# A written-out order of steps is replaced, and idle matmuls are put ahead of three stages

## The chip, the cores and the metric

One Trainium2 chip, and on it one core. A core has five engines that each run their own instruction stream in order: TensorE (PE, matmuls), VectorE (DVE), ScalarE (ACT), GpSimd (POOL) and SyncE (SP, which issues most transfers). They meet through semaphores. The metric is device time in microseconds of one execution; the median of three runs of the kernel before is 534.73 us (533.21 to 534.82).

## The reference

x has 2048 tokens of 128 features (4 batches of 512). Three layers act on it: half of a mixture of experts, a linear attention, and half of the same mixture again.

```python
x = x + 0.5 * ffn(layernorm(x)); x = x + attn(layernorm(x)); x = x + 0.5 * ffn(layernorm(x))

def ffn(x):    # 8 experts, 2 of them per token
    logits = (x @ gate_w + gate_b) / 0.9
    probs = softmax(logits where among the top 2, else -inf)
    h = gelu(einsum('bsd,edf->bsef', x, w1) + b1)             # 128 -> 512
    y = einsum('bse,bsed->bsd', probs, einsum('bsef,efd->bsed', h, w2) + b2)
    return layernorm(y) * ln_g + ln_b

def attn(x):   # 16 heads of 64, feature map elu + 1
    q, k, v = x @ wq + bq, x @ wk + bk, x @ wv + bv
    qm, km = elu(q) + 1, elu(k) + 1
    kv, z = einsum('nshd,nshm->nhmd', km, v), 1 / (einsum('nlhd,nhd->nlh', qm, km.sum(1)) + 1e-6)
    return einsum('nlhm,hmf->nlf', einsum('nlhd,nhmd,nlh->nlhm', qm, kv, z), wo) + bo
```

## The kernel before

The whole order of work is one list of words, ORDER (lines 65 to 113). A word is a step: its kind, then its arguments, where f1 is the first FFN, att the attention and f2 the second FFN. Each engine goes through the same list in the same order and takes from each step what is its part; so a word that moves, moves the step's instructions on every engine that has some, its DMA issues on SyncE among them. No scheduler stands behind it.

The tokens are worked on in four tiles of 512. In each FFN one tile is "dense": all eight experts are computed for it, as 16 units of half an expert (up.0 to up.15 and down.0 to down.15 in the first FFN, units 54 to 69 in the second). The other three tiles are "sparse": their tokens are scattered into blocks of 256 by expert, in DRAM (sorted1 and sorted2), and a block is one unit (units 16 to 34, and 35 to 53); a block beyond an expert's first gets its weights by a copy from W into Wd1 and Wd2, by a table made at run time. Results go to DRAM, and a gather brings two per token back.

A unit runs through four engines. xb: transposes of a loaded block on PE, a high part on ACT, a low part on DVE (matmuls are done in three products of high and low parts). up: 12 matmuls (6 in a dense unit), then the gelu on ACT, for dense units also the copy hh. low: DVE's low part hl. down: 12 matmuls (6) into one of two halves of psB. For a sparse unit then DVE's add of b2 (yT), yt: transposes on PE, a copy to yb on ACT, the store on SP. yb has two buffers, so ACT's copy of a unit waits for the store of the unit two before (L1088 to L1093), and down of a unit waits for the copy of the unit two before, which frees its half of psB (wait_bank, L707). mix: DVE adds a dense expert's gated result to acc.

Weights come in as stages: step W.u loads expert u's w1 and w2 (W.8 and W.9: wq and wk) into one of two stage buffers on SP; ACT copies the high part, Wl.u makes the low part on DVE, and only then may the stage after next be loaded. wv and wo load what is folded into VW. mix.u on SP reloads pb, the gate weights of the expert after next, once DVE's mix.u has freed it. fill1 (issued on ACT's queue) and fill (on SP) write zeros to sorted1 and sorted2. For fill, DVE first clears tok:

```python
sp.wait_ge(zero_ready, 2)
sp.dma_start(xs[1]..., zrow.unsqueeze(1).to_broadcast([P, 16, ROWS2 // 16])).then_inc(filled[1], 16)
```

The attention runs batch by batch: K.n.i and Q.n.j (products on PE, exponentials on ACT, Kf and Qf on DVE), kt and ksum (the sum of keys), kv (keys times normalised x, in psB), kvout (its copy, ACT), G (with VW), den and denz (the reciprocal of the denominator, DVE), z (spread over the heads by a matmul on zq), qz (DVE), out, oT, att. Between them stand, for tiles 1 to 3, the end of the first FFN (gather on POOL, top1 on ACT, comb, fstat and finish on DVE), the statistics of the next layernorm (stats on DVE, their root on POOL, norm on ACT), and the routing of the second FFN (gate, logits, top, route, slots, scatter). psA has two slots that up, K, Q, G, z, oT and some small steps use in turn.

On PE, SP and ACT the stores and copies of units 16 to 34 and the start of the attention stand so:

```python
act.wait_ge(y_stored[s % 2], 16 * (s // 2))     # L1092, step yt: ACT's copy to yb
pe.wait_ge(yb_ready, sparse_no(prior) + 1)      # L712, wait_bank: ahead of down
```

A kernel starts with 12 matmuls of ident on itself into psB (WARM_UP, L717), whose result is not used.

Of the kernel before, what the change touches and what calls it, by code (L numbers as in the profile page):

```python
# [69 lines left out]
top.f1.1.2 top.f1.1.3 route.f1.1.D low.4 consts picks down.2 scatter.f1.0 mix.1 table.f1 prep scatter.f1.1 scatter.f1.2  # L70
scatter.f1.3 scatter.f1.4 scatter.f1.5 scatter.f1.6 scatter.f1.7 scatter.f1.8 scatter.f1.9 scatter.f1.10 up.5 scatter.f1.11
exp.f1.1 W.5 Wl.4 low.5 wv down.3 slots.f1.1 up.6 mix.3 wo down.4 low.6 up.7 wvT.0.C W.6 Wl.5 up.8 down.5 mix.5 low.7 low.8 up.9
down.6 W.7 Wl.6 down.7 wvT.1.C mix.7 low.9 up.10 VW.0.C down.8 low.10 W.8 down.9 VW.1.C Wl.7 low.11 up.11 mix.9 up.12 VW.2.C
down.10 low.12 up.13 W.9 down.11 Wl.8 up.14 VW.3.C mix.11 low.13 down.12 low.14 up.15 Wl.9 down.13 bvwo.0.C mix.13 low.15
down.14 bvwo.1.C down.15 mix.15 xb.16 xb.17 up.16 xb.18 kbias low.16 up.17 xb.19 accT.f1.C shift.f1.0 fstat.f1.0 low.17 up.18
down.16 low.18 xb.20 up.19 xb.21 down.17 yt.16 low.19 up.20 finish.f1.0 xb.22 yt.17 down.18 stats.att.0 low.20 up.21 xb.23
norm.att.0 yt.18 low.21 up.22 down.19 xT.att.0.C down.20 xb.24 xl.att.0 yt.19 up.23 xb.25 low.22 soft.f1.1 down.21 yt.20 low.23
up.24 xb.26 shift.f1.1 down.22 yt.21 low.24 up.25 yt.22 down.23 xb.27 low.25 up.26 xb.28 shift.f1.2 down.24 yt.23 low.26 up.27
down.25 yt.24 xb.29 low.27 yt.25 up.28 xb.30 shift.f1.3 down.26 low.28 up.29 xb.31 up.30 yt.26 down.27 low.29 down.28 xb.32
yt.27 low.30 up.31 xb.33 yt.28 low.31 down.29 up.32 xb.34 yt.29 low.32 up.33 down.30 down.31 yt.30 low.33 down.32 up.34 yt.31  # L80
low.34 K.0.0 down.33 yt.32 down.34 yt.33 yt.34 gather.f1.1.0 gather.f1.1.1 K.0.1 gather.f1.1.2 gather.f1.1.3 Kf.0.0 fill Q.0.0
Kf.0.1 kt.0.1 kv.0.0 K.0.2 Qf.0.0 Kf.0.2 kt.0.2 Q.0.1 kv.0.1 K.0.3 Qf.0.1 Q.0.2 kv.0.2 Q.0.3 Kf.0.3 kt.0.3 Qf.0.2 Qf.0.3 kv.0.3
kvout.0 ksum.0 comb.f1.1 gs.0 top1.f1.1 fstat.f1.1 finish.f1.1 den.0.0 den.0.1 denz.0 stats.att.1 gather.f1.2.0 gather.f1.2.1
G.0 norm.att.1 z.0.0 qz.0.0 z.0.1 xT.att.1.A xl.att.1 qz.0.1 out.0.0 z.0.2 z.0.3 qz.0.2 K.1.0 out.0.1 gather.f1.2.2 qz.0.3
out.0.2 K.1.1 Kf.1.0 gather.f1.2.3 Kf.1.1 kt.1.1 outc.0 K.1.2 out.0.3 kv.1.0 top1.f1.2 comb.f1.2 fstat.f1.2 gather.f1.3.0 kv.1.1
K.1.3 Kf.1.2 kt.1.2 Q.1.0 Kf.1.3 kt.1.3 kv.1.2 Q.1.1 finish.f1.2 stats.att.2 gather.f1.3.1 Qf.1.0 Q.1.2 Qf.1.1 norm.att.2
gather.f1.3.2 gather.f1.3.3 Qf.1.2 Q.1.3 ksum.1 xT.att.2.A xl.att.2 Qf.1.3 gs.1 att.0 oT.0 K.2.0 top1.f1.3 comb.f1.3 den.1.0
kv.1.3 K.2.1 Kf.2.0 fstat.f1.3 K.2.2 finish.f1.3 Kf.2.1 kt.2.1 den.1.1 kv.2.0 stats.att.3 denz.1 stats.f2.0 kv.2.1 Kf.2.2 Kf.2.3
kvout.1 K.2.3 G.1 kt.2.2 kt.2.3 norm.att.3 xT.att.3.A xl.att.3 norm.f2.0 Q.2.0 z.1.0 qz.1.0 kv.2.2 z.1.1 qz.1.1 z.1.2 Qf.2.0
out.1.0 Q.2.1 qz.1.2 out.1.1 Qf.2.1 xl.f2.0 Q.2.2 z.1.3 qz.1.3 out.1.2 Qf.2.2 xT.f2.0.A Q.2.3 gate.f2.0.A logits.f2.0 out.1.3  # L90
top.f2.0.0 top.f2.0.1 kv.2.3 outc.1 Qf.2.3 top.f2.0.2 kvout.2 top.f2.0.3 route.f2.0.A slots.f2.0 scatter.f2.0 scatter.f2.1 K.3.0
Kf.3.0 ksum.2 gs.2 oT.1 att.1 scatter.f2.2 stats.f2.1 exp.f2.0 scatter.f2.3 den.2.0 den.2.1 denz.2 K.3.1 norm.f2.1 soft.f2.0
Kf.3.1 kt.3.1 K.3.2 kv.3.0 Kf.3.2 xl.f2.1 kv.3.1 xT.f2.1.A kt.3.2 G.2 K.3.3 z.2.0 qz.2.0 Kf.3.3 kt.3.3 qz.2.1 out.2.0
logits.f2.1 z.2.1 gate.f2.1.A out.2.1 z.2.2 qz.2.2 kv.3.2 top.f2.1.0 z.2.3 Q.3.0 qz.2.3 Q.3.1 out.2.2 out.2.3 outc.2 Qf.3.0
top.f2.1.1 top.f2.1.2 top.f2.1.3 route.f2.1.A Qf.3.1 oT.2 att.2 slots.f2.1 stats.f2.2 scatter.f2.4 scatter.f2.5 Q.3.2 Qf.3.2
scatter.f2.6 scatter.f2.7 Q.3.3 norm.f2.2 shift.f2.0 ksum.3 gs.3 kv.3.3 Qf.3.3 xT.f2.2.A xl.f2.2 den.3.0 kvout.3 gate.f2.2.A
logits.f2.2 den.3.1 top.f2.2.0 denz.3 G.3 top.f2.2.1 top.f2.2.2 scatter.f2.8 scatter.f2.9 scatter.f2.10 scatter.f2.11 z.3.0
top.f2.2.3 route.f2.2.A slots.f2.2 qz.3.0 z.3.1 qz.3.1 out.3.0 table.f2 dest.f2 exp.f2.1 exp.f2.2 outc.3 qz.3.2 out.3.1 z.3.2
z.3.3 qz.3.3 out.3.2 shift.f2.1 shift.f2.2 out.3.3 soft.f2.1 soft.f2.2 xb.35 xb.36 up.35 xb.37 low.35 up.36 xb.38 oT.3 att.3
up.37 low.36 xb.39 low.37 up.38 down.35 stats.f2.3 xb.40 low.38 down.36 yt.35 up.39 xb.41 norm.f2.3 down.37 yt.36 xb.42 low.39  # L100
up.40 yt.37 xl.f2.3 down.38 xT.f2.3.C low.40 up.41 down.39 yt.38 low.41 gate.f2.3.C xb.43 logits.f2.3 up.42 top.f2.3.0
top.f2.3.1 down.40 xb.44 low.42 up.43 yt.39 xb.45 top.f2.3.2 top.f2.3.3 exp.f2.3 up.44 yt.40 down.41 low.43 xb.46 soft.f2.3
shift.f2.3 down.42 yt.41 low.44 up.45 xb.47 probsT.f2.C down.43 yt.42 up.46 xb.48 low.45 yt.43 down.44 low.46 up.47 xb.49
down.45 yt.44 low.47 up.48 yt.45 low.48 down.46 xb.50 up.49 yt.46 xb.51 down.47 low.49 up.50 yt.47 xb.52 down.48 low.50 up.51
yt.48 xb.53 low.51 down.49 up.52 down.50 yt.49 low.52 down.51 yt.50 low.53 pb.f2 up.53 up.54 down.52 yt.51 low.54 up.55 down.53
yt.52 low.55 yt.53 up.56 down.54 low.56 up.57 gather.f2.0.0 gather.f2.0.1 gather.f2.0.2 gather.f2.0.3 down.55 mix.55 low.57
up.58 down.56 low.58 up.59 down.57 mix.57 gather.f2.1.0 low.59 up.60 top1.f2.0 comb.f2.0 down.58 low.60 up.61 gather.f2.1.1
gather.f2.1.2 fstat.f2.0 gather.f2.1.3 down.59 mix.59 up.62 low.61 finish.f2.0 gather.f2.2.0 gather.f2.2.1 gather.f2.2.2
gather.f2.2.3 mix.61 store.0 down.60 low.62 up.63 top1.f2.1 comb.f2.1 fstat.f2.1 down.61 low.63 up.64 low.64 up.65 store.1
down.62 low.65 down.63 mix.63 finish.f2.1 up.66 low.66 top1.f2.2 comb.f2.2 fstat.f2.2 down.64 up.67 down.65 mix.65 low.67  # L110
# [1542 lines left out]
```

## Time and profile before

| what | us |
|---|---|
| median of three runs | 534.73 |
| the profiled execution, its own time | 535.36 |
| its span, first to last instruction | 533.6 |
| PE busy | 423.0 (79%) |
| DVE busy | 364.1 (68%) |
| ACT busy | 277.0 (52%) |
| POOL busy | 165.7 (31%) |
| zero fill of sorted2 (7552 KB), issue to landing | 24.4 |

The profile is of one execution. Busy time counts matmuls, vector and scalar instructions; waiting is what lies between. PEclk is the share of full speed that TensorE's clock was granted: 1.00 is 2.4 GHz, 0.50 is 1.2 GHz, and a stretch in between held both. In a row of a timeline, the square brackets give how long the engine sat idle before the instruction and what ended that.

### The profile page before, as it was taken

Reading aid. Unit: us, or ns where it says so; the run is one execution under the profiler, and the core shown is the slowest. Engines: PE = TensorE matmul, PEld = TensorE weight load, DVE = VectorE, ACT = ScalarE, POOL = GpSimd, SP = SyncE. Lnnn points to the kernel's source line nnn. Section 1 sums busy time; section 2 is a strip of 40 time slices with the busy share of each in tenths; the row PEclk is TensorE's granted clock in tenths of the full one; section 3 lists DMA queues with packets and bytes.
Section 4 is the critical chain, followed back from the end, with each engine's and each line's share of the span. In section 5 each row is a group of like instructions: output and inputs, shape, how many; then the busy total and the mean of one; then the engine's idle time right before and its main releaser. Section 6 shows DMA issues by size and latency. Waiting matters only on the chain.

```text
span 533.6 us, 8029 instructions
## 1 busy us (share of the span) xinstructions
PE 423.0 (79%) x2559; PEld 335.2 (63%) x2559; DVE 364.1 (68%) x790; ACT 277.0 (52%) x560; POOL 165.7 (31%) x253
## 2 busy tenths in 40 slices
...
GB/s 172 77 79 267 193 124 128 110 250 126 235 256 174 88 371 251 25 15 11 31 0 1 1 31 11 0 11 35 84 209 215 225 230 234 119 76 73 80 79 20
DMA packets 50816, 62.92 MB, mean 118 GB/s; under 512 B 7772, under 2 KB 36821, under 8 KB 50775
## 3 DMA queue, kind: packets, MB, share of 16 engines
...
q14 instruction: 21, 0.16, 0.1%
...
## 4 chain that ended last, share of the span: by engine, by line
PE 24%; issue 18%; DVE 15%; POOL 10%; ACT 4%; DMA 2%; SPq 1%; POOLq 0%; DVEq 0%; ACTq 0%
POOL g L1592 4%; POOL sorted L1577 3%; PE psA L703 3%; PE psC L963 3%; PE psA L705 3%; PE psA L704 3%; PE psB L703 2%; PE psB L705 2%; PE psB L704 2%; DVE bst L1179 2%; POOL rstd L1559 2%; PE psB L914 2%; DVE hl L1354 2%; DVE hh L1351 1%; DMA results<-yb 1%
## 5 line engine op out<-in xcount | busy, mean ns | idle before, releaser
L1354 DVE TENSOR_TENSOR hl<-hid,hh 128x1024 fp32r<-128x1024 f32 x70 | 86.2, 1234 | 25.0 <-ACT hh L1086 19.9
L1079 ACT ACTIVATE hid<-psA,cols 128x512 f32<-128x512 f32 (+1 forms) x128 | 66.1, 580 | 21.9 <-PE psA L705 16.7
L1577 POOL DMA_INDIRECT sorted<-tok,di x48 | 49.6, 1033 | 72.8 <-DVE di L1329 59.3
L703 PE MATMUL psB<-hh,W 128*128 128x512 f32 (+1 forms) x128 | 47.9, 374 | 10.9 <-DVE hl L1354 9.8
L1592 POOL DMA_INDIRECT g<-results,di x24 | 27.2, 1135 | 65.2 <-DMA results<-yb 57.9
L1557 POOL TENSOR_SCALAR ve<-mv 128x4 f32<-128x4 f32 x20 | 7.0, 349 | 128.7 <-DVE mv L1182 128.1
L704 PE MATMUL psB<-hl,W 128*128 128x512 f32 (+1 forms) x128 | 45.0, 352 | 0.0
L705 PE MATMUL psB<-hh,W 128*128 128x512 f32 (+1 forms) x128 | 44.6, 349 | 0.0
L1592 POOL DMA_INDIRECT g<-results,dy x24 | 26.6, 1107 | 54.9 <-DMA results<-yb 48.0
L1079 ACT ACTIVATE hid<-psA,cols_d 128x256 f32<-128x256 f32 x88 | 34.7, 478 | 15.8 <-PE psA L705 11.2
L703 PEld LDWEIGHTS psB<-hh,W 128*128 128x128 f32 x128 | 25.7, 201 | 17.4 <-DVE hl L1354 13.1
L963 PE MATMUL psC<-qm,Gs 128*128 128x512 f32 x64 | 33.3, 658 | 4.1 <-DVE qm L1503 4.1
L1102 ACT ACTIVATE X<-psA,less 128x1024 f32<-128x1024 f32 x16 | 17.8, 1113 | 35.9 <-PE psA L895 35.9
L1086 ACT CAST hh<-hid 128x1024 fp32r<-128x1024 f32 x32 | 33.6, 1049 | 2.6
L1111 ACT ACTIVATE X<-psA,cols 128x512 f32<-128x512 f32 x32 | 22.1, 690 | 24.3 <-PE psA L705 23.1
L914 PE MATMUL psB<-km,xn 128*128 128x512 f32 x64 | 30.1, 598 | 3.6 <-DVE km L1452 2.4
L1339 DVE TENSOR_TENSOR xbl<-psC,xbh 128x256 fp32r<-128x256 f32 x38 | 16.0, 420 | 22.0 <-ACT xbh L1056 21.8
L703 PE MATMUL psA<-xh,W 128*128 128x512 f32 x64 | 28.0, 437 | 3.8 <-DVE xl L1230 3.4
L1351 DVE CAST hh<-hid 128x1024 fp32r<-128x1024 f32 x38 | 27.6, 727 | 4.0 <-ACT hid L1079 4.0
L703 PE MATMUL psB<-hh,Wd 128*128 128x256 f32 x88 | 26.8, 304 | 1.9 <-issue 1.8
L705 PEld LDWEIGHTS psB<-hh,W 128*128 128x128 f32 x128 | 25.6, 200 | 3.2
L1452 DVE SCALAR_TENSOR_TENSOR km<-X,psA 128x1024 f32<-128x1024 f32 x16 | 19.3, 1214 | 11.9 <-ACT X L1102 11.7
...
## 6 DMA issues: line engine op xcount, KB each, us to landing
Wd<-W SPq DMA_DIRECT2D x44, 512.0 KB, 3.1
sorted<-tok SPq DMA_DIRECT2D x1, 7552.0 KB, 24.4
...
```

Source lines behind the costliest of these rows:

```text
L703: nc.tensor.matmul(o, ah, bh, start=start, stop=False)
L704: nc.tensor.matmul(o, ah, bl, start=False, stop=False)
L705: return nc.tensor.matmul(o, al, bh, start=False, stop=stop)
L914: last = nc.tensor.matmul(psB[:, j, :], xn[:, n % 2, i, :], km[:, ti % 2, j * BANK:(j + 1) * BANK], start=(i == 0), stop=(i == ST - 1))
L963: last = nc.tensor.matmul(psC[:, 1, :], Gs[:, c, :], qm[:, c, :], start=(c == 0), stop=(c == HP - 1))
L1079: last = nc.scalar.activation(hid[:, u % 2, q * width:(q + 1) * width], ps(st)[:, q * width:(q + 1) * width], ACT.Gelu, bias=bias)
L1086: nc.scalar.copy(hh[:, u % HS, :], hid[:, u % 2, :]).then_inc(hh_ready, 1)
L1111: nc.scalar.activation(X[:, fslot(k), cs], ps(st)[:, cs], ACT.Exp, bias=bias)
L1351: link(nc.vector.tensor_copy(hh[:, u % HS, :], hid[:, u % 2, :]))
L1354: nc.vector.tensor_tensor(hl[:, u % HS, :], hid[:, u % 2, :], hh[:, u % HS, :].bitcast(F32), ALU.subtract)\
L1577: nc.gpsimd.indirect_dma_start(xs[ix(r)], bass.IndirectOffsetOnAxis(di[:, ix(r), k, j:j + 1], 0), tok[:, j, :], None)\
L1592: nc.gpsimd.indirect_dma_start(g[:, v, 2 * t + k, :], None, ys[ix(r)], bass.IndirectOffsetOnAxis(slots[:, k, off(r, n) + t:off(r, n) + t + ...
```

## The change

ORDER is replaced as a whole: the same words in another order, but for six new ones, heat.-1.0, heat.-1.1, heat.0.0, heat.0.1, heat.3.0 and heat.3.1. A heat step issues matmuls on PE whose result nobody reads: 6 of ident on itself (n = -1), or 4 of 512 columns with expert 0's weights (n = 0 and 3), into the second half of psB. For n of 0 or more it waits until kvout has read psB.

```diff
 ORDER = """
-W.0 stats.f1.0 norm.f1.0 W0.0 bias.A W0.1 xT.f1.0.C stats.f1.1 W.1 norm.f1.1 stats.f1.2 xl.f1.0 route_consts stats.f1.3
+W.0 stats.f1.0 W0.0 bias.A norm.f1.0 stats.f1.1 W0.1 W.1 stats.f1.2 xl.f1.0 stats.f1.3 norm.f1.1 xT.f1.0.C heat.-1.0 heat.-1.1
...
-    return [(kind, *(stages[v] if v in stages else int(v) if v.isdigit() else v for v in a))
+    return [(kind, *(stages[v] if v in stages else int(v) if v.lstrip('-').isdigit() else v for v in a))
...
+                elif kind == "heat":
+
+                    n, _ = a
+                    if n >= 0:
+                        pe.wait_ge(kxT_ready, n + 1)
+                        for _ in range(4):
+                            nc.tensor.matmul(psB[:, 1, :], W[:, 0, 0, 0, 0:P], W[:, 0, 1, 0, :], start=True, stop=True)
+                    else:
+                        for _ in range(6):
+                            nc.tensor.matmul(psB[:, 1, 0:P], ident[:, :], ident[:, :], start=True, stop=True)
```

SP at the end of the first FFN's sparse blocks, before: L692 is the store of a unit's result (step yt), L600 the load of a unit's second weights, L628 the fill, L554 the load of the second FFN's first block.

```order
L692 DMA results1<-yb 128x2x128 x3
L600 ISA
L600 DMA Wd2<-W 128x1024
L692 DMA results1<-yb 128x2x128 x5
L628 DMA sorted2<-tok 2048x1x944
L554 DMA xb<-sorted2 128x2x128
```

The same place now:

```order
L692 DMA results1<-yb 128x2x128
L600 ISA
L600 DMA Wd2<-W 128x1024
L692 DMA results1<-yb 128x2x128
L628 DMA sorted2<-tok 2048x1x944
L692 DMA results1<-yb 128x2x128 x5
L554 DMA xb<-sorted2 128x2x128
```

The fill has moved ahead of the last five stores, those of units 30 to 34. On DVE its memset of tok stands behind unit 34's xb.

SP in the first dense series, before, from the reload that takes the gate table: L652 is pb.0, L617 and L618 are a stage's w1 and w2 (W.4, then W.5), L658 a reload of pb (step mix), L631 wv, L636 wo.

```order
L652 DMA pb<-gate_table 128x512 x2
L617 DMA stage<-in_L_ffn_w_dram 128x512
L618 DMA stage<-in_L_ffn_w_dram 128x4x128
L658 DMA pb<-gate_table 128x512
L617 DMA stage<-in_L_ffn_w_dram 128x512
L618 DMA stage<-in_L_ffn_w_dram 128x4x128
L631 DMA wv_sb<-in_L_attn_wv_dram 128x1024
```

The same place now:

```order
L652 DMA pb<-gate_table 128x512 x2
L631 DMA wv_sb<-in_L_attn_wv_dram 128x1024
L617 DMA stage<-in_L_ffn_w_dram 128x512
L618 DMA stage<-in_L_ffn_w_dram 128x4x128
L617 DMA stage<-in_L_ffn_w_dram 128x512
L618 DMA stage<-in_L_ffn_w_dram 128x4x128
L658 DMA pb<-gate_table 128x512
```

W.5 has moved ahead of mix.1's reload, and wv ahead of W.4. On ACT, W.4 and W.5 stand behind the gelu of units 4 and 5.

DVE where the last routing of the second FFN meets batch 3's denominator, before: L1248 is the first step of top, L1489 to L1496 denz.3, L1434 G.3, L1250 to L1252 the second step of top.

```order
L1248 TENSOR_REDUCE gm<-gL 128x4
L1489 TENSOR_SCALAR oT<-psC 128x128
L1491 RECIPROCAL oT<-oT 128x128
L1492 CAST zh<-oT 128x128
L1496 SCALAR_TENSOR_TENSOR zq<-zh,lower,oT 32x128 x4
L1434 TENSOR_TENSOR Gs<-psA,Gs 128x1024
L1250 TENSOR_TENSOR gS<-gA,gm 128x32
L1251 SCALAR_TENSOR_TENSOR gX<-gS,gL 128x32
```

The same now, where lines behind the new branch have numbers larger by 10: L1336 to L1339 are the last rows of slots, L1499 to L1506 denz.3, L1444 G.3, L1513 qz, L1297 the table.

```order
L1336 TENSOR_REDUCE gm<-gX 128x4
L1338 CAST di<-gm 128x4
L1339 CAST di<-gm 128x4
L1499 TENSOR_SCALAR oT<-psC 128x128
L1501 RECIPROCAL oT<-oT 128x128
L1502 CAST zh<-oT 128x128
L1506 SCALAR_TENSOR_TENSOR zq<-zh,lower,oT 32x128 x4
L1444 TENSOR_TENSOR Gs<-psA,Gs 128x1024
L1513 TENSOR_TENSOR qm<-qm,psA 128x1024 x2
L1297 TENSOR_TENSOR gX<-pos,steps 128x40
```

All of top, route and slots has moved ahead of denz.3 and G.3.

## Rows read from the trace of the kernel before

**Rows 1.** Windows by stage: length, busy time of each engine, clock, DMA share, GB/s.
```profile
core 0: us, PE busy (x) PEld busy (x) DVE busy (x) ACT busy (x) POOL busy (x), PEclk, DMA share, GB/s
17.77:99.81 82.04, 67.32 (x309) 53.58 (x310) 56.83 (x117) 48.60 (x66) 40.85 (x108) 0.87 0.49 152
99.81:172.41 72.60, 60.67 (x473) 58.22 (x472) 56.25 (x101) 40.70 (x110) 13.25 (x11) 0.95 0.57 192
184.26:362.22 177.96, 144.14 (x814) 95.06 (x817) 112.82 (x244) 89.26 (x181) 58.51 (x69) 0.93 0.16 59
362.22:389.87 27.65, 15.69 (x116) 8.88 (x116) 20.04 (x70) 0.95 (x2) 13.42 (x15) 0.88 0.19 66
465.60:533.60 68.00, 45.48 (x185) 34.56 (x183) 45.25 (x106) 36.48 (x55) 31.61 (x32) 0.90 0.23 66
```

**Rows 2.** Waits of ACT, 17 to 100 us: total, times, longest.
```profile
ACT W L992 <- DMA stage<-in_L_ffn_w_dram: 18.7, 4, 7.6
```

**Rows 3.** Timeline of ACT, 34 to 60 us: start, length, instruction, idle before.
```profile
40.88 1.05 ACT L992 CAST W<-stage 128x1024 fp32r<-128x1024 f32 x1 [6.19 <-DMA stage<-in_L_ffn_w_dram]
...
54.15 1.04 ACT L992 CAST W<-stage 128x1024 fp32r<-128x1024 f32 x1 [7.62 <-DMA stage<-in_L_ffn_w_dram]
```

**Rows 4.** Timeline of PE around the first z product and batch 1's G.
```profile
206.67 1.97 PE L933 MATMUL psA<-VW,kxT 128*64 128x128 f32 x32
215.93 1.19 PE L952 MATMUL psA<-zq,pick 128*128 128x512 f32 x2 [7.29 <-DVE zq L1496]
...
281.81 3.58 PE L933 MATMUL psA<-VW,kxT 128*64 128x128 f32 x32 [2.58 <-DVE km L1452]
```

**Rows 5.** Timeline of POOL, 364 to 386 us.
```profile
371.86 0.96 POOL L1577 DMA_INDIRECT sorted<-tok,di  x1 [5.94 <-DVE di L1329]
```

**Rows 6.** Timeline of SP's issues, 355 to 394 us.
```profile
383.04 0.39 SPq L554 DMA_DIRECT2D xb<-sorted  x1
384.23 0.52 SPq L582 DMA_DIRECT2D Wd<-W  x1
384.88 0.51 SPq L587 DMA_DIRECT2D cols_d<-cols_e  x1
```

**Rows 7.** Timeline of SP's issues, 30 to 50 us.
```profile
35.51 0.43 SPq L617 DMA_DIRECT2D stage<-in_L_ffn_w_dram  x1
...
47.85 0.46 SPq L617 DMA_DIRECT2D stage<-in_L_ffn_w_dram  x1
```

**Rows 8.** Page, part 6: transfers, KB each, median us from issue to landing.
```profile
Wd<-W SPq DMA_DIRECT2D x44, 512.0 KB, 3.1
sorted<-tok SPq DMA_DIRECT2D x1, 7552.0 KB, 24.4
...
cols_d<-cols_e SPq DMA_DIRECT2D x22, 2.5 KB, 2.5
```

**Rows 9.** Timeline of PE, 0 to 18 us.
```profile
1.75 4.60 PE L718 MATMUL psB<-ident 128*128 128x128 f32 x24 [1.75 <-POOLq L1525]
...
17.77 0.77 PE L703 MATMUL psA<-xh,W 128*128 128x512 f32 x1 [3.41 <-DVE xl L1230]
```

**Rows 10.** Timeline of SP's issues, 160 to 190 us.
```profile
174.43 10.87 SPq L692 DMA_DIRECT2D results<-yb  x5
186.16 0.64 SPq L628 DMA_DIRECT2D sorted<-tok  x1
```

**Rows 11.** Timeline of DVE, 262 to 284 us.
```profile
266.38 1.23 DVE L1391 SCALAR_TENSOR_TENSOR g<-g,pr 128x128 f32<-128x128 f32 x4 [3.51 <-ACT g L1009]
```

**Rows 12.** Timeline of DVE, 355 to 386 us.
```profile
363.36 0.29 DVE L1489 TENSOR_SCALAR oT<-psC 128x128 f32<-128x128 f32 x1
...
367.53 0.18 DVE L1250 TENSOR_TENSOR gS<-gA,gm 128x32 f32<-128x32 f32 x1
```

**Rows 13.** Timeline of DVE, 500 to 534 us.
```profile
506.77 1.14 DVE L1421 SCALAR_TENSOR_TENSOR x<-g,rstd,x 128x128 f32<-128x128 f32 x4 [1.27 <-issue]
...
515.09 1.14 DVE L1415 SCALAR_TENSOR_TENSOR g<-g,mv,gain 128x128 f32<-128x128 f32 x4
...
522.68 0.89 DVE L1179 BATCH_NORM_STATS2 bst<-psC 128x6 f32<-128x128 f32 x4 [0.81 <-PE psC L857]
```

More of the change, by code:

```diff
@@ L70 @@
[L70 to L110, printed above, removed]
@@ L111 @@
-store.2 up.68 down.66 low.68 finish.f2.2 up.69 down.67 low.69 down.68 down.69 mix.67 mix.69 accT.f2.C fstat.f2.3 finish.f2.3
-store.3
+W.0 stats.f1.0 W0.0 bias.A norm.f1.0 stats.f1.1 W0.1 W.1 stats.f1.2 xl.f1.0 stats.f1.3 norm.f1.1 xT.f1.0.C heat.-1.0 heat.-1.1
+up.0 xT.f1.1.C gate.f1.0.D route_consts W.2 Wl.1 up.1 xl.f1.1 xl.f1.2 logits.f1.0 gate.f1.1.D xT.f1.2.C norm.f1.2 top.f1.0.0
+norm.f1.3 up.2 xT.f1.3.C top.f1.0.1 up.3 gate.f1.2.D down.0 top.f1.0.2 low.0 Wl.2 top.f1.0.3 logits.f1.1 low.1 gate.f1.3.D
@@ new lines @@
+Qf.0.2 Qf.0.3 gather.f1.2.0 comb.f1.1 ksum.0 fstat.f1.1 top1.f1.1 kv.0.3 kvout.0 finish.f1.1 stats.att.1 gs.0 denz.0 den.0.0
+den.0.1 gather.f1.2.1 G.0 heat.0.1 heat.0.0 z.0.0 qz.0.0 qz.0.1 norm.att.1 z.0.1 gather.f1.2.2 xT.att.1.A z.0.2 out.0.0 out.0.1
+z.0.3 xl.att.1 K.1.0 K.1.1 top1.f1.2 out.0.2 gather.f1.2.3 out.0.3 K.1.2 kv.1.0 qz.0.2 qz.0.3 K.1.3 kv.1.1 Kf.1.0 outc.0 Q.1.0
+Q.1.1 Kf.1.1 ksum.1 comb.f1.2 kt.1.1 fstat.f1.2 gather.f1.3.0 finish.f1.2 stats.att.2 Kf.1.2 kt.1.2 Kf.1.3 kt.1.3 Qf.1.0
```

43 lines of the change are left out of this document (40 added, 3 removed).

## The prediction

> **What bounds the kernel now.** I read the busy time of each engine stage by stage first, then who waits for whom and the stretches in order of time, and last the transfers. I cut the execution at the starts of instructions that begin a stage [rows 1]. In the first dense series (17.8 to 99.8) TensorE is busy 67.3 of 82.0 us, in the sparse blocks of the first FFN (to the end of unit 30's down, 172.4) 60.7 of 72.6, from batch 0's second K product (184.3) to the last gate logits of the attention part 144.1 of 178.0, in the crossing to the second FFN 15.7 of 27.7, and in the last dense series with the tail 45.5 of 68.0. No engine is full. What an order can win is TensorE's idle time: 14.7, 11.9, 33.8, 12.0 and 22.5 us; what it can lose is any wait that it makes on a queue.
>
> A few waits set most of that idle time. ScalarE waits 18.7 us in four waits for weight stages in the first series [rows 2], the two longest 6.19 and 7.62 us [rows 3]. TensorE waits 7.29 us for the input of the first z product, and 2.58 us for key features ahead of batch 1's G, which then takes 3.58 us against batch 0's 1.97: half clock [rows 4]. GpSimd waits 5.94 us for slots ahead of the last scatters [rows 5], and the second FFN's first block is loaded behind them [rows 6].
>
> **The change part by part.**
>
> *First dense series: -11 us, between 0 and -15.* W.4's load is issued at 35.51, W.5's only at 47.85 [rows 7], because mix.1's reload of pb, which waits for VectorE, stands ahead of it. So ScalarE gets W.5 at 54.15, and unit 6's activation follows at 55.2 [rows 3]. In the new order wv, W.4 and W.5 stand right behind pb.0, ahead of mix.1. In flight then are pb, wv, W.4 and W.5, 0.5 MB each, and fill1's 2.4 MB, now issued earlier on ScalarE's queue: 4.4 MB. The kernel's largest transfer moves 7.55 MB in 24.4 us, 0.31 MB/us [rows 8], so they need 14 us from about 33.5: W.5 lands near 47.5 and unit 6 is activated near 48.5, -6.7. Later stages hang on the same chain (W.6 behind mix.3, W.7 behind mix.5), and W.6 now stands behind unit 8 on ScalarE, which covers its wait: some 4 more of the 18.7. If transfers side by side are slower than that one row, nothing is won; more than the idle 14.7 cannot be.
>
> *Heat ahead of up.0: 0.* Twelve matmuls on ident cost what the twelve at the program's start do, 4.60 us at half clock; TensorE now waits 3.41 us there, and the gate product, which stands ahead of up.0 now, moves behind it [rows 9]. up.0 starts a little earlier and with the clock up, but ScalarE's stages set the pace afterwards, so this is inside the -11. Uncovered, it would cost 4.6.
>
> *Sparse blocks of the first FFN: -2, between 0 and -4.* accT moves ahead of up.17, so SyncE, which waits for it before it loads the second weights, goes on earlier. Then TensorE is near full. Unit 30's down ends at 172.4 - 13 = 159.4.
>
> *The fill: +20.5, between +3 and +22.* On this step hangs the sign. On SyncE the zero fill of sorted2 moves from behind the last five stores to ahead of them. Now the five stores begin at 174.43 and the fill is issued at 186.16 [rows 10]; it takes 24.4 us to land [rows 8]. SyncE's transfers land in the order of issue: a cols_d copy of 2.5 KB, issued 0.65 us behind a Wd of 512 KB [rows 6], lands 2.5 us after its issue in the median and that Wd 3.1 after its own [rows 8]: the same moment. So a store behind the fill lands behind the fill. ScalarE's copy of unit 32 waits for unit 30's store (yb has two buffers), unit 34's down waits for that copy's bank, and behind both in program order stand batch 0's key products. From the end T of unit 30's down: the fill's memset stands behind unit 34's block split, so I put the issue at T + 2.2 (an estimate: transposes, split, memset); landing T + 26.6; then the copy, the down, its yT and two pairs of transposes, about 4.2 at half clock (an estimate from the two G rows' ratio): K.0.1 starts at T + 30.8. Now it starts at 184.26, T + 11.9 [rows 1]. That is +18.9, and 1.6 for K.0.1 itself at half clock, like G. The lower end holds if stores share the engines with the fill instead of queueing; the upper if the clock stays down longer.
>
> The rows say that SyncE's transfers land in order. The Trainium skill's page "DMA: Bandwidth & Descriptors" (section "Queues, rings and completion order") says that on each of the 16 DMA engines descriptors are consumed in ring order, but that completion is not first-in first-out per issuing engine. By the first half a store waits out the fill, which is the term above; by the second it could be done early where the fill does not use its rings, which is the lower end. The trace agrees with the first half (the two medians); no run here shows the second.
>
> *Attention: -12, between -4 and -17.* Three places and a rest. Key features of batch 2 stand ahead of stats.f2.0 on VectorE, so that G.1 loses its 2.58 wait and its half clock, 1.61 [rows 4]: -4.2. Gathers of tiles 2 and 3 no longer stand behind late statistics, so the combine that VectorE waits 3.51 us for [rows 11] is ready: -3.5. Heat keeps TensorE going ahead of z.0.0, so out of batch 0 runs nearer to full clock: -2; the eight matmuls cost at most 0.77 each [rows 9], 6.2 us, inside the wait of 7.29 [rows 4], and put z off only where that wait shrinks below them. Of that wait top1.0.1, which goes ahead of kvout and gs, takes some: -2.3. The lower end is G alone; the upper all of 2.58, 1.61, 3.51 and 7.29, 15, and the 2 of the clock.
>
> *Crossing: -4, between -2 and -6.* The routing of tile 2 moves ahead of denz.3 and G.3 on VectorE, which stand in its way from 363.36 to 367.53 [rows 12]: 4.2 us. The last eight scatters start when the slots are there [rows 5]. Late next is out.3.3, as z.3 moves back by as much; but dest.f2 moves behind qz.3.3, so that it ends about when it does now. The second heat stands ahead of z.3.0 while denz.3 runs: 0; uncovered, up to 6.2.
>
> *Tail: -3, between -1 and -4.* finish.2.2 (two rows of 1.14 from 515.09) moves behind mix.69, where VectorE sits idle 0.81 us for accT, and finish.2.1 loses its wait of 1.27, since GpSimd now takes its statistics ahead of the last gathers [rows 13].
>
> **Sum.** -11 - 2 + 20.5 - 12 - 4 - 3 = -11.5. Against the profiled execution's own 535.4 us that is 523.9; it lies 0.6 above the median of the runs, 534.73. I say 523.5.
>
> **Rivals.** *The fill is not paid back* (slower). Its place is ScalarE's copy of unit 32, its price 20.5, and it decides once the other terms win less than that. With -6 in the first series, nothing in the sparse blocks, -5 in the attention, -2 and -1 behind it, the sum is +6.5: 541. For it: my gains are sums of small terms, and each holds only where no other wait is next. Against it: ScalarE's two waits stand plainly in the rows. Chance 0.24.
>
> *The stores are not held* (much faster). With +3 in place of +20.5 the sum is -29: 506. For it: nothing of SyncE's stands behind the one fill in this trace. Against it: 22 pairs of Wd and cols_d. Chance 0.07.
>
> *The attention gain is hidden.* If the second FFN's scatters start no earlier, since the statistics of tiles 1 and 2 stand behind scatters 0 to 3 in GpSimd's queue now, attention gives -2 or so and the sum is about -1.5: 534. For it: GpSimd is in the chain at the crossing [rows 5]. Against it: it has 119 us free of the stage's 178 [rows 1]. Chance 0.08.
>
> **Numbers.** The forecast has 0.61, with its own range 513 to 532. The range that takes in most of the slow rival is 511 to 540. A measurement of this kernel tells no change from 0.3%, 1.6 us. Faster: 0.61 + 0.07 = 0.68; the same 0.08; slower 0.24.
>
> **What would show it.** In the profile after: ScalarE's stage of W.5 before 49 and unit 6's activation behind it; one wait of about 20 us of ScalarE's yb copy for a store, TensorE idle beside it and slow K matmuls behind; no wait of 5.94 on GpSimd; the last finish right behind accT. The prediction is wrong if that yb wait is missing or under 10 us, if the first series ends later than 93, or if the stretch from K.0.1's start to the second FFN's first up is not at least 8 us shorter than now (184.26 to 389.87, 205.6).

## The result and the profile after

The changed kernel takes 518.22 us in the median (516.69 to 521.72, four runs) against 533.97 for the kernel before (532.53 to 534.82). The ratio is 0.9717, 95% interval 0.9655 to 0.9779. The forecast was 523.5. A later set of the same kernel gave 520.42 (ratio 0.9776, 0.9755 to 0.9797), so the gain lies between 12 and 16 us.

The profiled execution took 516.69 us, with a span of 514.9, 18.7 less than before. That is 2.9 more than the medians differ by: this execution is the shortest of its set, and the profiled one of before (535.36) lies 1.4 above its median. First its windows by stage, cut at the same instructions as [rows 1]: up.0, unit 16's xb, the end of unit 30's down, K.0.1, unit 35's up, unit 54's up, the end. Columns as there.

```profile
core 0: us, PE busy (x) PEld busy (x) DVE busy (x) ACT busy (x) POOL busy (x), PEclk, DMA share, GB/s
15.10:88.27 73.17, 61.00 (x304) 48.15 (x303) 54.42 (x110) 49.30 (x66) 42.46 (x105) 0.95 0.52 152
88.27:158.10 69.83, 60.69 (x472) 57.84 (x473) 54.86 (x96) 39.09 (x105) 11.31 (x11) 0.95 0.64 218
158.10:186.01 27.91, 14.06 (x95) 12.65 (x93) 9.97 (x15) 7.39 (x16) 0.00 (x0) 0.76 0.82 315
186.01:367.57 181.56, 159.11 (x940) 103.08 (x940) 129.71 (x304) 89.28 (x183) 71.01 (x84) 0.96 0.08 23
367.57:436.62 69.05, 64.28 (x519) 61.77 (x518) 54.92 (x111) 44.35 (x117) 3.49 (x6) 0.98 0.66 224
436.62:514.90 78.28, 54.82 (x229) 42.13 (x227) 50.07 (x113) 41.83 (x64) 35.65 (x32) 0.86 0.24 68
```

The same cuts of the kernel before, where [rows 1] has other ends:

```profile
172.41:184.26 11.85, 10.47 (x79) 9.47 (x78) 6.42 (x10) 5.35 (x10) 0.00 (x0) 1.00 0.23 77
184.26:389.87 205.61, 159.83 (x926) 103.94 (x926) 132.86 (x313) 90.20 (x183) 71.94 (x84) 0.93 0.17 60
389.87:458.64 68.77, 64.74 (x517) 62.51 (x517) 53.24 (x102) 43.30 (x115) 4.39 (x6) 0.95 0.64 220
458.64:533.60 74.96, 52.08 (x228) 40.41 (x226) 49.67 (x111) 42.73 (x67) 31.61 (x32) 0.91 0.25 71
```

Set side by side: up to the first sparse block 88.27 instead of 99.81 (-11.5); sparse blocks -2.8; from unit 30's down to K.0.1 27.9 instead of 11.9 (+16.1); from K.0.1 to unit 35's up 181.6 instead of 205.6 (-24.1); second sparse blocks +0.3; from unit 54's up to the end 78.3 instead of 75.0 (+3.3). The sum is -18.7. So one stage gives back 16 of what the others win, and the tail is slower, not faster.

*The first series.* The timeline of ScalarE (start, length, instruction, idle before) has both weight stages close together now; W.5 starts 8.6 us earlier than in [rows 3]; its load is issued at 37.28 instead of 47.85 [rows 7].

```profile
43.45 1.04 ACT L1002 CAST W<-stage 128x1024 fp32r<-128x1024 f32 x1 [5.85 <-DMA stage<-in_L_ffn_w_dram]
45.58 1.04 ACT L1002 CAST W<-stage 128x1024 fp32r<-128x1024 f32 x1 [1.09 <-DMA stage<-in_L_ffn_w_dram]
```

The waits of ScalarE for weight stages, in all of the first series, were 18.7 us [rows 2]:

```profile
ACT W L1002 <- DMA stage<-in_L_ffn_w_dram: 7.7, 3, 5.8
```

*The fill.* SyncE issues it 2.1 us behind the end of unit 30's down, ahead of five stores [rows 10]; the transfer table then gives its time to landing, which was 24.4 [rows 8]; ScalarE's timeline has the wait that follows.

```profile
160.21 0.64 SPq L628 DMA_DIRECT2D sorted<-tok  x1
160.89 26.17 SPq L692 DMA_DIRECT2D results<-yb  x5
```

```profile
sorted<-tok SPq DMA_DIRECT2D x1, 7552.0 KB, 21.2
```

```profile
166.01 0.39 ACT L1103 COPY yb<-psB 128x256 f32<-128x256 f32 x1
...
181.87 0.37 ACT L1103 COPY yb<-psB 128x256 f32<-128x256 f32 x1 [13.05 <-DMA results<-yb]
```

The fill lands at 160.21 + 21.2 = 181.4, and ScalarE's copy of unit 32, which waits for the store issued just behind it, starts 0.5 us later. TensorE sits idle for 13.5 us in the same place.

*The attention.* Batch 1's G waits 0.21 us instead of 2.58 and takes 1.97 at full clock; the first z product waits 3.48 us behind the heat instead of 7.29, but at half clock (2.38 us for four, 0.60 each, where 0.35 is full) [rows 4].

```profile
217.08 2.38 PE L952 MATMUL psA<-zq,pick 128*128 128x512 f32 x4 [3.48 <-DVE zq L1506]
...
271.56 1.97 PE L933 MATMUL psA<-VW,kxT 128*64 128x128 f32 x32 [0.21 <-DVE km L1462]
```

VectorE's combine of tile 3, which waited 3.51 us [rows 11], waits for nothing:

```profile
256.90 1.17 DVE L1401 SCALAR_TENSOR_TENSOR g<-g,pr 128x128 f32<-128x128 f32 x4
```

*The crossing.* On GpSimd the wait ahead of the last scatters is 1.99 us instead of 5.94 [rows 5], and on VectorE denz.3 stands right behind the last row of slots [rows 12].

```profile
352.45 0.95 POOL L1587 DMA_INDIRECT sorted<-tok,di  x1 [1.99 <-DVE di L1339]
```

```profile
352.01 0.16 DVE L1339 CAST di<-gm 128x4 int32<-128x4 f32 x1
352.08 0.28 DVE L1499 TENSOR_SCALAR oT<-psC 128x128 f32<-128x128 f32 x1
```

*The tail.* Three views tell of it. GpSimd's statistics of tile 0 stand among the gathers:

```profile
462.53 1.62 POOL L1602 DMA_INDIRECT g<-results,dy  x1 [0.30 <-DVE mv L1192]
464.22 0.55 POOL L1567 TENSOR_SCALAR ve<-mv 128x4 f32<-128x4 f32 x1
464.85 2.03 POOL L1573 TENSOR_TENSOR rstd<-ve,half 128x4 f32<-128x4 f32 x1
467.08 1.06 POOL L1602 DMA_INDIRECT g<-results,dy  x1 [0.20 <-issue]
```

ScalarE's top1 (L1019) waits for gathers, ahead of the gelus of units 64 and of 68 and 69:

```profile
472.33 0.40 ACT L1019 ACTIVATE g<-g,pr 128x128 f32<-128x128 f32 x1 [3.32 <-DMA g<-results,dy]
474.57 0.40 ACT L1019 ACTIVATE g<-g,pr 128x128 f32<-128x128 f32 x1 [1.83 <-DMA g<-results,dy]
...
491.15 0.40 ACT L1019 ACTIVATE g<-g,pr 128x128 f32<-128x128 f32 x1 [3.89 <-DMA g<-results,dy]
491.45 1.25 ACT L1089 ACTIVATE hid<-psA,cols 128x512 f32<-128x512 f32 x2
```

TensorE waits for the low parts of units 62, 63 and 68. VectorE makes that of 62 behind the finish of tile 0, that of 63 behind the combine of tile 1, which waits for the top1 rows above, and that of 68 behind its late gelu:

```profile
470.91 0.50 PE L703 MATMUL psB<-hh,W 128*128 128x512 f32 x1 [1.84 <-DVE hl L1364]
476.67 0.79 PE L703 MATMUL psB<-hh,W 128*128 128x512 f32 x1 [2.73 <-DVE hl L1364]
495.25 0.51 PE L703 MATMUL psB<-hh,W 128*128 128x512 f32 x1 [3.05 <-DVE hl L1364]
```

At the very end finish.2.2 (the first two rows) stands between mix.69 and the last statistics, so these start at 504.01, 1.4 us after TensorE's accT has ended at 502.64. In [rows 13] they start 0.04 us after accT's end at 522.64:

```profile
501.79 1.13 DVE L1425 SCALAR_TENSOR_TENSOR g<-g,mv,gain 128x128 f32<-128x128 f32 x4
502.95 1.14 DVE L1431 SCALAR_TENSOR_TENSOR x<-g,rstd,x 128x128 f32<-128x128 f32 x4
504.01 0.88 DVE L1189 BATCH_NORM_STATS2 bst<-psC 128x6 f32<-128x128 f32 x4
```

### The profile page after: what moved, and what is told of

Read it like the earlier page. It is cut to its first block, busy times and chain, and to the rows that moved or that the text cites. A ratio compares the mean times of both kernels' runs of the same rounds, so it can differ in the third digit from the quotient of the medians.

```text
span 514.9 us, 8106 instructions
## 1 busy us (share of the span) xinstructions
PE 424.6 (82%) x2599; PEld 335.9 (65%) x2599; DVE 363.6 (71%) x790; ACT 276.4 (54%) x560; POOL 169.7 (33%) x253
## 4 chain that ended last, share of the span: by engine, by line
PE 26%; issue 15%; DVE 13%; POOL 11%; DMA 4%; ACT 4%; SPq 2%; POOLq 0%; DVEq 0%; ACTq 0%
POOL sorted L1587 4%; POOL g L1602 4%; PE psA L703 4%; PE psA L705 3%; PE psA L704 3%; PE psB L703 3%; PE psB L704 2%; PE psB L705 2%; PE psC L963 2%; DVE bst L1189 2%; DVE km L1462 2%; PE psB L914 1%; DMA g<-results,dy 1%; DMA results<-yb 1%; DVE x L1431 1%
## 5 line engine op out<-in xcount | busy, mean ns | idle before, releaser
L1089 ACT ACTIVATE hid<-psA,cols 128x512 f32<-128x512 f32 (+1 forms) x128 | 66.0, 581 | 24.9 <-DVE hl L1364 13.0
L1587 POOL DMA_INDIRECT sorted<-tok,di x48 | 54.4, 1133 | 49.9 <-DVE di L1339 36.2
L703 PE MATMUL psB<-hh,W 128*128 128x512 f32 (+1 forms) x128 | 46.8, 365 | 9.9 <-DVE hl L1364 9.5
L1602 POOL DMA_INDIRECT g<-results,di x24 | 24.4, 1015 | 78.5 <-DMA results<-yb 71.3
L1602 POOL DMA_INDIRECT g<-results,dy x24 | 28.6, 1192 | 52.6 <-DMA results<-yb 45.8
L705 PE MATMUL psB<-hh,W 128*128 128x512 f32 (+1 forms) x128 | 44.2, 346 | 0.0
L1089 ACT ACTIVATE hid<-psA,cols_d 128x256 f32<-128x256 f32 x88 | 34.5, 478 | 15.5 <-PE psA L705 12.9
L703 PE MATMUL psB<-hh,Wd 128*128 128x256 f32 x88 | 26.7, 303 | 17.2 <-issue 13.9
L703 PEld LDWEIGHTS psB<-hh,W 128*128 128x128 f32 x128 | 25.0, 196 | 17.0 <-DVE hl L1364 14.5
L1066 ACT CAST xbh<-psC 128x256 fp32r<-128x256 f32 x38 | 14.6, 384 | 38.0 <-PE psC L780 36.6
L914 PE MATMUL psB<-km,xn 128*128 128x512 f32 x64 | 31.6, 625 | 0.0
L1462 DVE SCALAR_TENSOR_TENSOR qm<-X,R 128x1024 f32<-128x1024 f32 x16 | 19.5, 1221 | 16.6 <-ACT R L1122 16.5
L963 PE MATMUL psC<-qm,Gs 128*128 128x512 f32 x64 | 30.5, 610 | 0.9 <-DVE qm L1513 0.9
L1103 ACT COPY yb<-psB 128x256 f32<-128x256 f32 x38 | 14.3, 379 | 29.3 <-DMA results<-yb 15.2
## 6 DMA issues: line engine op xcount, KB each, us to landing
sorted<-tok SPq DMA_DIRECT2D x1, 7552.0 KB, 21.2
```

The costliest lines, as they stand in the source:

```text
L703: nc.tensor.matmul(o, ah, bh, start=start, stop=False)
L705: return nc.tensor.matmul(o, al, bh, start=False, stop=stop)
L914: last = nc.tensor.matmul(psB[:, j, :], xn[:, n % 2, i, :], km[:, ti % 2, j * BANK:(j + 1) * BANK], start=(i == 0), stop=(i == ST - 1))
L1089: last = nc.scalar.activation(hid[:, u % 2, q * width:(q + 1) * width], ps(st)[:, q * width:(q + 1) * width], ACT.Gelu, bias=bias)
L1462: nc.vector.scalar_tensor_tensor(dst, X[:, fslot(k), :], 1.0, linear, ALU.min, ALU.max if kind == "Kf" else ALU.add)\
L1587: nc.gpsimd.indirect_dma_start(xs[ix(r)], bass.IndirectOffsetOnAxis(di[:, ix(r), k, j:j + 1], 0), tok[:, j, :], None)\
```

## The experiments

Every kernel below is the changed one or the one before with one edit, e8 and e12 with two and three. Medians are of four to six runs, ratios are to the kernel before on the same chip. The lengths of the stages come from the profiles, read as differences of the starts and ends of the same instructions (us):

| kernel | to unit 16's xb | sparse blocks | down.30 to K.0.1 | K.0.1 to up.35 | up.35 to up.54 | up.54 to last finish | median |
|---|---|---|---|---|---|---|---|
| before | 99.8 | 72.6 | 11.9 | 205.6 | 68.8 | 68.0 | 534 |
| changed | 88.3 | 69.8 | 27.9 | 181.6 | 69.1 | 71.4 | 518.22 |
| e1 fill back | 87.5 | 69.3 | 13.2 | 183.4 | 69.6 | 73.0 | 504.24 |
| e2 fill on ScalarE's queue | 87.4 | 69.5 | 13.9 | 185.4 | 69.0 | 70.5 | 506.51 |
| e7 before, fill moved | 99.2 | 72.6 | 26.5 | 205.8 | 68.7 | 67.7 | 547.77 |
| e4 no heat | 88.7 | 70.6 | 29.2 | 184.5 | 69.6 | 70.9 | 524.05 |
| e3 before, new front | 89.0 | 75.8 | 11.8 | 202.8 | 68.8 | 67.8 | 525.35 |
| e5 before, new attention | 99.6 | 72.6 | 11.8 | 183.9 | 71.3 | 67.8 | 515.96 |
| e6 old tail | 87.8 | 69.6 | 29.2 | 184.0 | 69.0 | 67.9 | 517.03 |
| e8 fill back, old tail | 88.4 | 69.5 | 13.2 | 183.1 | 68.9 | 67.2 | 502.27 |
| e12 e8 with longer heat | 87.7 | 69.7 | 13.2 | 179.2 | 68.7 | 67.8 | 497.22 |

### The fill: e1, e2 and e7

e1 moves one word of the changed kernel's ORDER:

```diff
-... xb.34 yt.29 fill low.32 gather.f1.1.0 ... yt.33 yt.34 K.0.1 ...
+... xb.34 yt.29 low.32 gather.f1.1.0 ... yt.33 yt.34 fill K.0.1 ...
```

> The changed kernel with one word moved: fill stands behind yt.34 again, so SyncE issues the stores of units 30 to 34 ahead of it. Theory (the stores wait out the fill in SyncE's queue): the 13.0 us wait of ScalarE's yb copy goes, from the end of unit 30's down to K.0.1 it takes about 12 us again instead of 27.9, the first gathers then run beside the fill and give back about 2; 16 - 2 = 14 off 518.2, so about 504. Rival (the time is only pushed on: the gathers of tile 1 beside the fill make the end of the first FFN late, and the attention waits for it): the start comes as early, but the stretch from K.0.1 to unit 35's up grows from 181.6 by 8 us or more, and the whole is 512 or slower.

It took 504.24 us, ratio 0.9452 (0.9425 to 0.9478). The stage is down from 27.9 to 13.2, and the stretch behind it grew by 1.8 only. The theory holds; the rival falls.

e2 leaves the word where the change put it, and lets ScalarE issue the fill:

```diff
-                    sp.wait_ge(zero_ready, 2)
+                    act.wait_ge(zero_ready, 2)
...
-                    sp.dma_start(xs[1]...
+                    act.dma_start(xs[1]...
```

> The changed kernel with the fill at its new place, but issued on ScalarE's queue instead of SyncE's. Theory (order within SyncE's queue holds the stores): the five stores land in under 9 us each beside the fill, ScalarE's longest wait for a store falls from 13.0 to under 5, and the whole is about 508. Rival (the fill fills the DMA engines or the memory, whatever the queue): the stores still take about 20 us, the wait stays above 10, and the whole is within 3 us of 518.

It took 506.51 us, ratio 0.9513 (0.9482 to 0.9543). The transfers issued from 156 to 190 us (KB each, median us from issue to landing) show why:

```profile
sorted<-tok ACTq DMA_DIRECT2D x1, 7552.0 KB, 24.9
results<-yb SPq DMA_DIRECT2D x6, 128.0 KB, 7.7
```

ScalarE's waits for stores in that kernel, total, times and longest, from 140 to 215 us:

```profile
ACT yb L1103 <- DMA results<-yb: 7.7, 3, 4.8
```

The same fill moves the same bytes at the same time, and a store beside it now lands in 7.7 us (median of six, 4.6 to 8.3); behind it in SyncE's queue the first two took 20.9 and 12.7, both landing within 0.9 us of the fill. So it is the queue that holds them. Sharing the engines costs a store some 5 us over the 2.7 of its median, not 18. The Trainium skill's page "DMA: Bandwidth & Descriptors" (section "Queues, rings and completion order") says that each DMA engine takes turns between the queues that have work for it, and consumes each ring in order. Both halves agree with these two kernels (7.7 us beside the fill, 20.9 and 12.7 behind it).

e7 moves the fill alone, in the kernel before:

```diff
-... yt.29 low.32 up.33 ... gather.f1.1.3 Kf.0.0 fill Q.0.0 ...
+... yt.29 fill low.32 up.33 ... gather.f1.1.3 Kf.0.0 Q.0.0 ...
```

> The kernel before with one word moved: fill stands ahead of yt.30, as in the changed kernel. Theory: the stretch from the end of unit 30's down to K.0.1 grows from 11.9 to 27 or 28 us, ScalarE waits 12 us or more for a store, the gathers land faster; 534 + 16 - 2 = 548. Rival (in the changed kernel something else of the new order, not the fill, made that stretch long): within 3 us of 534.

It took 547.77 us, ratio 1.0253 (1.0224 to 1.0282): 14 slower, and ScalarE waits 13.3 us for a store. The one word is enough; nothing else of the new order is needed.

```profile
193.94 0.37 ACT L1093 COPY yb<-psB 128x256 f32<-128x256 f32 x1 [13.32 <-DMA results<-yb]
```

### The stretches by themselves: e3 and e5

e3 is the kernel before with the first 149 words of the new order, to xb.17, and e5 the kernel before with the new words from behind G.0 to down.37 (at these places both orders have done the same steps).

> The kernel before with the new order up to step xb.17 alone (with the heat ahead of up.0). Theory: the first dense series ends 11.5 us earlier, as in the changed kernel, and nothing behind it takes that back: 534.0 - 11.5 = 522.5. Rival (the second sparse loads or the zero fill wait for something that did not move, so that part of it is lost again): 526 or slower.

It took 525.35, ratio 0.9869 (0.9846 to 0.9891): 7 us, not 11.5, and so between the theory (522.5) and the rival (526 or slower). The profile puts unit 16's xb at 89.0, 10.8 earlier, so the front does alone what it does in the changed kernel; but the sparse blocks in the old order take 3.2 us more. Part of that is a wait of TensorE for the normalised x of batch 0, 4.18 us against 2.62 before:

```profile
122.45 1.09 PE L732 MATMUL psC<-ident,xn 128*128 128x128 f32 x4 [4.18 <-ACT xn L1036]
```

So by this one profile the -2.8 of the sparse blocks in the changed kernel is worth more than it looks: the new order there also keeps the front's gain. The same profile is 2.8 us shorter from K.0.1 to unit 35's up, where no word has moved, and its span is 10.6 below that of before; which stages make the 7 us of the medians stays open.

> The kernel before with the new order from the step behind G.0 to step norm of the second FFN's dense tile (the attention from its first z product on and the crossing, with the heat of batches 0 and 3). Theory: from K.0.1 to unit 35's up it takes 182 to 185 us instead of 205.6, and the whole is about 534 - 22 = 512. Rival (the gain there needs the early zero fill, which lets the gathers of the first FFN run alone): 520 or slower.

It took 515.96, ratio 0.9692 (0.9671 to 0.9713): 16.5 us, midway between the theory (512) and the rival's bound (520). The stretch itself came out as expected (183.9), with the fill late; so the rival, that the gain needs an early fill, falls by the stage. Some 2.5 us are given back in the second sparse blocks (71.3 against 68.8), by what I did not follow up.

### The tail: e6 and e8

e6 is the changed kernel with its last 92 words, from up.54 on, in the order of before.

> The changed kernel with the words from up.54 to the end in the order of before. Theory (the new tail lost time, because GpSimd's and ScalarE's steps for the first two tiles stand between the gathers and ahead of the last two gelus): from up.54's start to the end 75 us instead of 78.3, so 515. Rival (the last gathers set the end in either order): 518 within 1 us.

In the profile the stretch from up.54 to the end of the last finish falls from 71.4 to 67.9, so by the stage the theory holds. The table bears it out: the seven kernels with the old tail have 67.2 to 68.0 there, the four with the new one 70.5 to 73.0. The time is 517.03 (513.15 to 519.68), ratio 0.9714 (0.9678 to 0.9750): 1.2 below the first set of the changed kernel, which is within the rival's bound, and 3.4 below the second set. Its interval overlaps that of the first set and ends just below that of the second (0.9755), so the times alone don't settle it. And since e6 moves all the words of the tail, it doesn't show which of them costs what.

e8 takes e1 and e6 together.

> The changed kernel with fill behind yt.34 and the words from up.54 on in the order of before. Theory: both gains add up, 518.2 - 14 - 3.3 = 501. Rival (the second FFN's scatters or the tail take back what the early start gives): 506 or slower.

502.27 us, ratio 0.9436 (0.9401 to 0.9471), near the 501 of the theory; the stage gains add up (13.2 and 67.2). In the times the old tail gives 2.0 us over e1, and the two intervals overlap.

### The heat: e4, e9, e10, e11 and e12

e4 drops all six heat words, e10 the two with -1, e11 the four of batches 0 and 3; e9 is the changed kernel once more.

> The changed kernel without its six heat words. Theory of the prediction (they cost nothing and give about 2 us after the first z product): the half clock that the kernel before shows from 213.5 to 227.1 comes back behind z.0.0, and the whole is 1 to 4 us slower, 519 to 522. Rival (the gain of the attention part is the clock that the heat keeps up): 526 or slower. Other rival (the clock stays up without them): 518 within 1 us.

524.05, ratio 0.9831 (0.9798 to 0.9864): 5.8 slower than the changed kernel of the first set: between the theory (519 to 522) and the first rival (526 or slower), so it settles neither, and the next three take the heat apart.

> The changed kernel as it is, beside the next two, so that the heat is judged on one chip: 518, with single runs from 516 to 522.

> The changed kernel without heat.-1.0 and heat.-1.1 (the 12 matmuls on ident ahead of up.0). Without any heat it was 5.8 us slower (524.05 against 518.22, of two sets of runs). Theory (ScalarE's stages set the pace of the first series, so this heat changes nothing): within 1.5 us of the changed kernel. Rival (the difference was this heat's): 3 to 6 us slower than the changed kernel.

> The changed kernel without the heat of batches 0 and 3 (16 matmuls). Theory (the half clock behind the first z product lasts longer without it, 10.5 us against 8.5 in the profiles so far, and the second place gains nothing): 1 to 3 us slower than the changed kernel. Rival (the whole 5.8 us was theirs): 4 to 6 us slower. Other rival (the difference between the two sets was their spread): within 1 us.

On one chip: 520.42 for the changed kernel (0.9755 to 0.9797), 523.50 without the heat on ident (0.9772 to 0.9838), 517.55 without the heat of batches 0 and 3 (0.9684 to 0.9728). So e10 is 3.1 slower, at the edge of its rival (3 to 6) and outside its theory, and e11 is 2.9 faster, which none of its three expectations had. Windows from the start of up.0 to up.3 of the changed kernel and of e10 show what the first heat buys:

```profile
15.10:23.19 8.09, 7.44 (x49) 6.25 (x48) 6.20 (x23) 6.50 (x9) 4.56 (x70) 1.00 0.24 69
```

```profile
13.22:26.45 13.23, 13.23 (x47) 11.28 (x47) 10.70 (x38) 7.71 (x11) 8.18 (x74) 0.51 0.23 61
```

Without it up.0 starts 1.9 us earlier, but e10's first units run at half clock, up.3 starts 3.3 later, and so does all of the series up to unit 16's xb (91.6 against 88.3). In the profile of e4 the clock rose at 16.2 us, and unit 16's xb came at 88.7; the nine profiles of kernels with this heat have it at 87.4 to 89.2, so there the heat would have bought nothing. Nor does the heat settle the clock: in the second profile of the changed kernel (e9) TensorE is at half clock from 9.3 to 12.7 us and again from 26.3 to 33.2. In the times it is worth more: e4 and e11 differ in this heat alone, and their ratios, 0.9831 (0.9798 to 0.9864) and 0.9706 (0.9684 to 0.9728), lie clearly apart, though they come from two chips. By these pairs it gives some 3 to 6.5 us in the median (the intervals of e9 and e10 overlap), of which the profiles show at most 3.4, in the first series; where the rest lies stays open.

The heat of batch 0 gains nothing that can be shown. With it TensorE still waits 3.48 us for the first z product and is then at half clock, as without it (5.52 us in e11). The heat of batch 3 does better: with it TensorE waits 0.50 us for z.3.0, stays at full clock, and takes 12.9 us from there to the end of out.3.3; in e11 it waits 2.56, has half clock behind the first product, and takes 13.6. The times don't show this gain. The kernel without the 16 matmuls is 0.7% faster than the changed kernel on this chip, with the intervals apart; the interval of the first set (0.9655 to 0.9779) takes in both. The profile of e11 is of its slowest run (520.55 us) and has the span of e9's (518.8 and 518.6), so whether the matmuls cost something, and where, stays open.

e12 is e8 with a longer heat for batch 0:

```diff
-                        for _ in range(4):
+                        for _ in range(9 if n == 0 else 4):
```

> The version with fill behind yt.34 and the old tail (502.27), with 9 instead of 4 matmuls in each heat step of batch 0, 18 in all: some 4.9 us of the 5.5 that TensorE has between G.0 and the first z product. Theory (the clock falls there because TensorE still waits 3.5 us behind the short heat): no half clock behind z.0.0, the stretch from z.0.0 to K.1.0 falls from 9.9 to about 8 and with it the whole by 2 to 3, to 499 or 500. Rival (the clock falls there whatever the heat does): half clock in the same place, 502 or slower.

It took 497.22 us, ratio 0.9346 (0.9315 to 0.9376), the fastest of all; e8, on another chip, has 0.9436 (0.9401 to 0.9471). That is more than the theory's 2 to 3 us. TensorE's timeline, e8 first, then e12 (L971 is the heat):

```profile
196.55 2.11 PE L971 MATMUL psB<-W 128*128 128x512 f32 x8
202.14 0.75 PE L952 MATMUL psA<-zq,pick 128*128 128x512 f32 x2 [3.48 <-DVE zq L1506]
203.30 1.22 PE L952 MATMUL psA<-zq,pick 128*128 128x512 f32 x2 [0.41 <-DVE Gs L1444]
...
206.86 4.90 PE L963 MATMUL psC<-qm,Gs 128*128 128x512 f32 x8
```

```profile
196.12 4.38 PE L971 MATMUL psB<-W 128*128 128x512 f32 x18
201.71 0.70 PE L952 MATMUL psA<-zq,pick 128*128 128x512 f32 x2 [1.21 <-DVE zq L1506]
202.88 0.74 PE L952 MATMUL psA<-zq,pick 128*128 128x512 f32 x2 [0.46 <-DVE Gs L1444]
...
205.71 3.59 PE L963 MATMUL psC<-qm,Gs 128*128 128x512 f32 x8
```

With 1.21 us of idle left the clock stays up: the second pair of z products takes 0.74 us instead of 1.22, and from the first z product to K.1.0 it takes 7.9 us instead of 9.9. In the other nine profiles with this order of words around z.0.0 it takes 9.2 to 11.4. That is 2 of the 5 us by which the medians differ; another 1.5 lie between K.3.0 and the last out of batch 2, where this profile has less half clock, and the rest I can't place.

## Why the prediction was right, and where it was not

*The sum.* Forecast -11.5, measured -18.7 in the profile and -15.8 in the medians; sign and range were right. That the sum came as near is in part luck: the fill, the attention, the crossing and the first two stages came out 13.7 us better than forecast, the tail and the second sparse blocks 6.6 worse.

*First series, -11:* 11.5. The way is the forecast one: W.5 at 45.58 ("before 49"), 7.7 us of waiting for stages instead of 18.7. W.4 and W.5 landed at 43.4 and 45.6, earlier than the 47.5 that I had from the fill's rate. e3 shows the term by itself in the profile (10.8). *Sparse blocks, -2:* 2.8; that it came by the earlier loads of the forecast is not shown.

*The fill, +20.5:* the mechanism was right at every step (e1, e2 and e7), the size was not: 16.1, and ScalarE's wait 13.0 where I wrote about 20. The issue came at T + 2.1 (forecast 2.2), and from the landing to K.0.1 it took 4.65 (4.2). What failed are two parts of the term. I took 24.4 us for the landing from a fill beside which gathers ran (in e1, where they do again, it is 24.1); with the stores held behind it, it took 21.2, and 21.1 to 22.4 in the six other profiles of that kind. And I charged 1.6 for a K.0.1 at half clock; half clock fell on unit 34's down (2.90 us), and K.0.1 ran in 2.09. The wait was shorter than 20 also because ScalarE had the exponentials of K.0.0 to do until 168.8.

*Attention, -12:* 16.4 (162.6 to 146.2 us from K.0.1 to the end of out.2.3). Two of the three places were right, G.1 and the combine. The largest piece lies between K.2.0 and K.3.0, 47.95 to 39.29:

```profile
261.24:309.19 47.95, 41.00 (x216) 26.23 (x217) 33.53 (x76) 23.58 (x43) 7.18 (x12) 0.93 0.02 5
```

```profile
257.54:296.83 39.29, 36.84 (x200) 23.67 (x197) 31.77 (x81) 21.41 (x40) 5.03 (x10) 1.00 0.00 1
```

TensorE's idle time falls from 6.95 to 2.45 us and its busy time by 4.2, of which 2.0 is kv.1.3, now ahead of K.2.0, and the rest full clock. I had counted G.1 alone. What I had for the third place, z.0.0, was wrong. The heat was to give full clock behind it: the mechanism is there (e12), but eight matmuls left 3.48 us of idle. That the stretch from z.0.0 to K.1.0 takes 9.4 us instead of 11.8, close to the 2 of the forecast, comes at half clock, with waits of 1.14 and 1.56 us gone. And of the 2.3 us ahead of z.0.0 only 0.6 came (K.0.1 to z.0.0, 31.7 to 31.1).

*Crossing, -4:* 7.6 (43.0 to 35.4 from out.2.3's end to unit 35's up). From the end of den.3.1 to z.3.0 it takes 6.6 us instead of 3.3: z.3 moves back by what the slots take, as forecast. What I missed lies behind it. From z.3.0 to the end of out.3.3 it takes 12.9 instead of 19.5, since VectorE goes from G.3 to the qz steps without the routing in between, and TensorE loses the waits of 2.25, 2.56 and 2.26 us that it had there (timeline of before, below); and unit 35's up, with its block there earlier, follows out.3.3 at once, where it came 3.9 us later before.

```profile
369.46 0.18 PE L751 MATMUL psA<-M,before 128*128 128x32 bf16 x1 [2.25 <-issue]
...
372.76 1.22 PE L952 MATMUL psA<-zq,pick 128*128 128x512 f32 x2 [2.56 <-DVE qm L1503]
...
382.31 3.70 PE L963 MATMUL psC<-qm,Gs 128*128 128x512 f32 x8 [2.26 <-DVE qm L1503]
```

*Tail, -3:* +3.3, the step with the wrong sign. The early statistics on GpSimd were counted as a wait that VectorE loses (1.27), not as 2.7 and 1.3 us in the queue of the gathers, where one step of 1.35 stood before. The gathers now take 39.5 us from first to last instead of 34.9 (some of it in longer issues of single gathers, which I did not follow up); behind these wait ScalarE's top1 and, behind that, VectorE's combine and the last gelus. And finish.2.2, moved behind mix.69 "into idle time" of 0.81, takes 2.3 there, 1.4 of it on the path. e6 shows the stretch's 3.5 come back, for all of these moves together.

*Heat ahead of up.0, 0:* not nothing: 3 to 6.5 us in the medians (e4, e10 and e11), at most 3.4 of it seen in the first series. The price was misread too: the 4.60 us of [rows 9] stand at full clock (PEclk 1.00 from 1.75 to 6.35 us), and the new twelve took 5.26 at half clock (0.50 from 10.00 to 15.10); the wait covered all but 1.9 of it.

*The rivals.* That the fill is not paid back set its price at 20.5, which came out at 16.1, and what pays it back at 14, which came out at 34.8. That the stores are not held is refuted (e1, e7). That the attention gain is hidden is refuted by e5.

*The signs to look for.* The yb wait, the first series and the stretch from K.0.1 came out as named; slow K matmuls and a last finish right behind accT did not.
